# A guessed top-k threshold: its update rewritten over kept points, and GpSimd's copies cut in four

## What is computed

```python
def _topk_attention(Q, K, V, topk):          # 16 heads, d = 16, topk = 64
    scores = jnp.einsum('bhqd,bhkd->bhqk', Q, K) / jnp.sqrt(jnp.asarray(d, Q.dtype))
    topk_scores, topk_idx = jax.lax.top_k(scores, topk)
    probs = jax.nn.softmax(topk_scores, axis=-1)
    ...
x = x + tanh(g_xattn) * attention(layernorm(x), ctx, ctx)
x = x + tanh(g_ffn) * fp8_linear(layernorm(x))
```

## Time and profile before

| | us |
|---|---|
| median of 3 runs | 3022.32 |
| lowest, highest | 3021.08, 3029.27 |
| the profiled execution: its own time | 3019.36 |
| its span, first to last instruction | 3017.5 |
| VectorE busy in it | 2564.5 |
| ScalarE busy in it | 2500.6 |

### The profile page before, as it was taken

One profiled execution on the slowest core, in us unless ns is written; L12 is line 12 of the kernel. 1 busy time (PEld: TensorE's weight loads), 2 busy tenths in 40 slices (PEclk: granted clock), 3 DMA queues, 4 the chain that ended last, 5 costly groups with the idle time before them and its releaser, 6 DMA issues. The chain is left out here.

```text
span 3017.5 us, 56335 instructions
## 1 busy us (share of the span) xinstructions
PE 1434.2 (48%) x9104; PEld 920.2 (30%) x9104; DVE 2564.5 (85%) x10738; ACT 2500.6 (83%) x8774; POOL 1007.2 (33%) x1204
## 2 busy tenths in 40 slices
PE   3345555445544545433445445554445345445443
PEld 2123333333322333322333233332233233233321
DVE  1688899888989898888888889988988888898884
ACT  1679999799988899957989799998799699697982
POOL 5223343233434233422333334332343233232112
PEclk8556676666666776666766576766666676666656
DMA  4323333223333323232223333323233223232111
GB/s 69 48 39 64 61 57 59 49 57 63 68 57 52 62 57 63 55 54 42 54 56 66 57 65 56 63 57 61 53 61 64 44 52 63 46 65 44 36 37 33
DMA packets 451929, 166.76 MB, mean 55 GB/s; under 512 B 245616, under 2 KB 451440, under 8 KB 451520
## 3 DMA queue, kind: packets, MB, share of 16 engines
q1 hardware_dynamic: 451136, 162.38, 30.2%
q0 software_dynamic: 384, 0.33, 0.1%
HBM read 102.57 MB, written 59.24 MB: 54 GB/s over the span
## 5 line engine op out<-in xcount | busy, mean ns | idle before, releaser
L971 ACT ACTIVATE act_junk<-score_sb,X 128x256 int8<-128x256 f32 x3072 | 1522.1, 509 | 141.3 <-DVE X L1293 60.2
L971 ACT ACTIVATION_READ_ACCUMULATOR act_junk<-score_sb,X 128x1 f32 x3072 | 621.9, 202 | 0.0
L1006 ACT ACTIVATE unfit<-score_sb,thr 128x256 bf16<-128x256 f32 x1024 | 431.1, 514 | 169.5 <-DVEq L1444 169.5
L759 PE MATMUL ps_s<-ks,qs 96*128 96x256 bf16 x1024 | 231.8, 347 | 610.6 <-DVE score_sb L1179 600.6
L773 PE MATMUL ps_e<-qs,ks 99*128 99x256 bf16 x1024 | 348.9, 352 | 275.1 <-ACT unfit L1006 185.5
L1179 DVE TENSOR_SCALAR_CACHE_REDUCE score_sb<-ps_s 128x256 f32<-128x256 f32 x1024 | 397.9, 411 | 16.3 <-PE ps_s L759 10.8
L777 PE MATMUL ps_e<-dropb,unfit 128*128 128x128 bf16 x2048 | 350.4, 270 | 0.0
L1015 ACT ACTIVATE pT_sb<-ps_e 128x512 f32<-128x512 f32 x512 | 302.6, 592 | 51.6 <-PE ps_e L777 50.9
L794 PE MATMUL ps_o<-pT_sb,v_aug 128*32 128x256 f32 x2048 | 285.9, 499 | 110.2 <-ACT pT_sb L1015 59.2
L567 POOL CAST split<-proj 128x512 bf16<-128x512 f32 x64 | 46.5, 727 | 862.8 <-ACT proj L955 862.3
L1317 DVE TENSOR_SCALAR_CACHE_REDUCE masked<-score_sb,X 128x256 f32<-128x256 f32 x768 | 318.8, 470 | 13.9 <-DVE x_res L1497 8.4
(11 more groups left out here) (181 smaller groups left out, 3843.5 us busy)
## 6 DMA issues: line engine op xcount, KB each, us to landing
rows<-q_scr SPq DMA_DIRECT2D x192, 128.0 KB, 5.0
rows<-k_scr SPq DMA_DIRECT2D x192, 128.0 KB, 4.9
o_scr<-o_sb SPq DMA_DIRECT2D x128, 128.0 KB, 2.8
q_scr<-split SPq DMA_DIRECT2D x32, 384.0 KB, 2.7
k_scr<-split SPq DMA_DIRECT2D x32, 384.0 KB, 2.7
x_in<-in_x SPq DMA_DIRECT2D x32, 256.0 KB, 2.8
ctx_sb<-in_ctx SPq DMA_DIRECT2D x32, 256.0 KB, 3.0
v_scr<-proj SPq DMA_DIRECT2D x32, 256.0 KB, 5.9
```

The costliest lines, as they stand in the source:

```text
L759: ins = nc.tensor.matmul(ps_s[:, n % 2, jh * TOK:(jh + 1) * TOK], qs[u][0:SPLITS, h, 8 * jh:8 * jh + 8, :].rearrange("d j t -> d (j t)"), ...
L971: ins = nc.scalar.activation(act_junk[:, t % JUNK, :], score_sb[:, slot, t, :], ACT.Sign, scale=-1.0, bias=X[slot % 2][:, 0, t:t + 1], acc ...
L1006: ins = nc.scalar.activation(unfit[:, n % MASKS, jh, :], score_sb[:, slot, t, :], ACT.Relu, scale=-1.0, bias=thr[:, slot, t:t + 1])
```

## The change

The bracket and its tiles (`A`, `B`, `AB`, `above`, `below`, `far`, `both`) are gone. Instead each group keeps the three guesses and distances of its rounds (`guess`, one slot a round), and an update picks from these:

- round 0: three instructions; every row makes the Newton step, near rows too;
- round 1: ten; the chord through points 0 and 1 where they lie on both sides, else the Newton step from point 1; near rows move too;
- round 2: thirteen; the chord from point 2 to point 1 if that lies on the other side, else to point 0, else the Newton step. Rows near at point 2 keep it. The result is written straight into `following`, so the copy of line 1314 is gone.

A distance of round r has r times 2^-6 added (APART), so that two points never have equal distances. SLOPE goes from 0.0115 / 2 to 0.0123 / 2. The final tiles and the final counts wait for a semaphore of their own (`s_last`) and read the guess in `following`. The last step of round 2 has two waits ahead of it, for ScalarE's final counts and VectorE's picks of the group before.

GpSimd copies the operands by head in four pieces, each with 4 of the 16 blocks j of a row. The three small instructions of `prepare_rounding` that mark rows out of range (lines 1481, 1483, 1485) move from VectorE to GpSimd, behind its rounding (line 636) and ahead of the maxima's split; `finish` waits for them there (`s_nn`).

```diff
@@ -50,15 +50,17 @@
 AIM = 60.5
 WINDOW = 8
 START = 0.6745
-SLOPE = 0.0115 / 2
+SLOPE = 0.0123 / 2
 ROOT_BITS = 532487669.0
-NO_POINT = 1000.0
+APART = 2.0 ** -6
 WIDE = ((0, 1, 2, 3), (6, 7, 8, 9), (12, 13, 14, 15))
 NARROW = ((4, 5), (10, 11), ())
 HEADS = ((0, 1, 2), (3, 4, 5), (6, 7))
 QUARTER = 4
-FINAL_BEFORE = (0, 14, 27)
-FINAL = 45
+FINAL_BEFORE = (0, 13, 26)
+FINAL = 44
+PICKED = 41
+FCS = 4

...
@@ -123,21 +125,15 @@
         max8 = sb("max8", [P, 8])


-        X = [sb(f"X{k}", [P, 2, GT]) for k in range(2)]
-        A = [sb(f"A{k}", [P, 2, GT]) for k in range(2)]
-        B = [sb(f"B{k}", [P, 2, GT]) for k in range(2)]
-        AB = sb("AB", [P, 2, GT])
+        guess = [sb(f"guess{k}", [P, GUIDES, 2, GT]) for k in range(2)]
         count = [sb(f"count{k}", [P, GT]) for k in range(2)]
-        aim = sb("aim", [P, GT])
-        newton = sb("newton", [P, GT])
-        product = sb("product", [P, GT])
+        step = sb("step", [P, GT])
+        product = sb("product", [P, GUIDES, GT])
+        limits = sb("limits", [P, GUIDES, GT])
+        flags = sb("flags", [P, GUIDES, GT], I32)
+        across = sb("across", [P, GT], I32)
+        run = product[:, 0:2, :]
         chord = sb("chord", [P, GT])
-        square = sb("square", [P, GT])
-        above = sb("above", [P, 2, GT], I32)
-        below = sb("below", [P, 2, GT], I32)
-        far = sb("far", [P, GT], I32)
-        far_f = sb("far_f", [P, GT])
-        both = sb("both", [P, GT], I32)
...
@@ -510,7 +508,8 @@
             nc.gpsimd.memset(ones_c[:], 1.0).then_inc(s_id, 1)
             nc.gpsimd.memset(ones_r[:], 1.0).then_inc(s_id, 1)

-            nc.gpsimd.memset(aim[:], TOK - 2 * AIM).then_inc(s_id, 1)
+            nc.gpsimd.memset(limits[:, 0:2, :], 0.0).then_inc(s_id, 1)
+            nc.gpsimd.memset(limits[:, 2, :], (WINDOW - 1) ** 2 + 0.5).then_inc(s_id, 1)
...
-                nc.gpsimd.tensor_copy((qs, ks)[k][u][0:SPLITS].rearrange("d h j t -> d j h t"),
-                                      rows[:].rearrange("d j (h t) -> d j h t", t=D)).then_inc((s_qh, s_kh)[k], 1)
+                for j in range(0, NJ, NJ // 4):
+                    ins = nc.gpsimd.tensor_copy((qs, ks)[k][u][0:SPLITS, :, j:j + NJ // 4, :].rearrange("d h j t -> d j h t"),
+                                                rows[:, j:j + NJ // 4, :].rearrange("d j (h t) -> d j h t", t=D))
+                ins.then_inc((s_qh, s_kh)[k], 1)
...
                 nc.gpsimd.tensor_tensor(xq_sb[:], ysum_sb, magic_sb[:], ALU.subtract).then_inc(s_q, 1)
+                pool.wait_ge(s_nan, 2 * b + 2)
+                carry(pool)
+                nc.gpsimd.tensor_scalar(nanrow[:], rowmax[:], 464.0, 3.0e38, ALU.is_gt, ALU.mult).then_inc(s_nn, 1)
+                pool.wait_ge(s_nn, 3 * b + 1)
+                carry(pool)
+                nc.gpsimd.tensor_scalar(nanrow[:], nanrow[:], 3.0e38, None, ALU.mult).then_inc(s_nn, 1)
+                pool.wait_ge(s_nn, 3 * b + 2)
+                carry(pool)
+                nc.gpsimd.tensor_tensor(rowmax[:], nanrow[:], nanrow[:], ALU.subtract).then_inc(s_nn, 1)
...
-                                               bias=X[slot % 2][:, 0, t:t + 1], accum_out=count[slot % 2][:, t:t + 1])
+                                               bias=guess[slot % 2][:, r, 0, t:t + 1], accum_out=count[slot % 2][:, t:t + 1])
...
             def final_counts(i, slot, r, counted):

-                act.wait_ge(s_fin, FINAL * i + 1)
+                act.wait_ge(s_last, i + 1)
                 act.wait_ge(s_cnt, counted)
                 for t in NARROW[r]:
                     ins = nc.scalar.activation(act_junk[:, t % JUNK, :], score_sb[:, slot, t, :], ACT.Sign, scale=-1.0,
-                                               bias=X[slot % 2][:, 0, t:t + 1], accum_out=final_count[:, t:t + 1])
+                                               bias=following[:, t, 0:1], accum_out=final_count[:, t:t + 1])
...
                 nc.vector.tensor_reduce(variance[:], gauss_sq, AX.X, ALU.add).then_inc(s_st, 1)
-                nc.vector.memset(A[slot % 2][:], NO_POINT)
-                nc.vector.memset(B[slot % 2][:], -NO_POINT)
...
-                nc.vector.scalar_tensor_tensor(x[:, 0, :], sd[:], START, gauss_mean[:], ALU.mult, ALU.add).then_inc(s_st, 1)
+                nc.vector.scalar_tensor_tensor(guess[slot % 2][:, 0, 0, :], sd[:], START, gauss_mean[:], ALU.mult, ALU.add).then_inc(s_st, 1)
...
             def update_thresholds(i, slot, r):
-
-
-                x = X[slot % 2]
-                lo_side, hi_side = A[slot % 2], B[slot % 2]
-                off = x[:, 1:2, :].to_broadcast([P, 2, GT])
+                points = guess[slot % 2]
+                x, off = points[:, r, 0, :], points[:, r, 1, :]
                 dve.wait_ge(s_cnt, GT * (GUIDES * i + r + 1))
                 carry(dve)
-                nc.vector.tensor_tensor(x[:, 1, :], aim[:], count[slot % 2][:], ALU.subtract).then_inc(s_upd, 1)
+                nc.vector.tensor_scalar(off, count[slot % 2][:], -1.0, TOK - 2 * AIM + r * APART, ALU.mult,
+                                        ALU.add).then_inc(s_upd, 1)
                 yield
                 dve.wait_ge(s_upd, 1)
-                nc.vector.tensor_scalar(above[:], off, 0.0, None, ALU.is_gt)
-                nc.vector.tensor_scalar(below[:], off, 0.0, None, ALU.is_le)
-                nc.vector.tensor_tensor(square[:], x[:, 1, :], x[:, 1, :], ALU.mult)
-                nc.vector.scalar_tensor_tensor(newton[:], x[:, 1, :], SLOPE, spread[slot % 2][:], ALU.mult,
+                if r == 1:
+                    nc.vector.tensor_tensor(product[:, 2, :], points[:, 0, 1, :], off, ALU.mult)
+                    nc.vector.tensor_tensor(run, points[:, 1], points[:, 0], ALU.subtract)
+                if r == 2:
+                    nc.vector.tensor_tensor(product[:], points[:, :, 1, :], points[:, 2:3, 1, :].to_broadcast([P, GUIDES, GT]),
+                                            ALU.mult)
+                nc.vector.scalar_tensor_tensor(step[:], off, SLOPE, spread[slot % 2][:], ALU.mult,
                                                ALU.mult).then_inc(s_upd, 1)
                 yield
-                dve.wait_ge(s_upd, 2)
-                nc.vector.copy_predicated(lo_side[:], above[:], x[:])
-                nc.vector.copy_predicated(hi_side[:], below[:], x[:])
-                nc.vector.tensor_tensor(newton[:], newton[:], x[:, 0, :], ALU.add)
-                if r:
-                    nc.vector.tensor_scalar(far_f[:], square[:], (WINDOW - 1) ** 2 + 0.5, None, ALU.is_gt)
-                nc.vector.tensor_scalar(far[:], square[:], (WINDOW - 1) ** 2 + 0.5, None, ALU.is_gt).then_inc(s_upd, 1)
-                yield
-                dve.wait_ge(s_upd, 3)
-                ins = nc.vector.copy_predicated(x[:, 0, :], far[:], newton[:])
+                done = 2
+                dve.wait_ge(s_upd, done)
                 if r == 0:
-                    ins.then_inc(s_thr, 1)
+                    nc.vector.tensor_tensor(points[:, 1, 0, :], x, step[:], ALU.add).then_inc(s_thr, 1)
                     dve.sem_clear(s_upd)
                     return
-                nc.vector.tensor_tensor(AB[:], hi_side[:], lo_side[:], ALU.subtract).then_inc(s_upd, 1)
+                if r == 1:
+                    nc.vector.tensor_scalar(across[:], product[:, 2, :], 0.0, None, ALU.is_lt)
+                if r == 2:
+                    nc.vector.tensor_tensor(flags[:], product[:], limits[:], ALU.is_lt).then_inc(s_upd, 1)
+                    yield
+                    dve.wait_ge(s_upd, 3)
+                    nc.vector.copy_predicated(points[:, 0], flags[:, 1:2, :].to_broadcast([P, 2, GT]), points[:, 1])
+                    nc.vector.tensor_tensor(across[:], flags[:, 0, :], flags[:, 1, :], ALU.max).then_inc(s_upd, 1)
+                    yield
+                    dve.wait_ge(s_upd, 4)
+                    nc.vector.tensor_tensor(run, points[:, 2], points[:, 0], ALU.subtract).then_inc(s_upd, 1)
+                    yield
+                    done = 5
+                    dve.wait_ge(s_upd, done)
+                nc.vector.reciprocal(chord[:], run[:, 1, :])
+                nc.vector.scalar_tensor_tensor(run[:, 0, :], run[:, 0, :], -1.0, off, ALU.mult, ALU.mult).then_inc(s_upd, 1)
                 yield
-                dve.wait_ge(s_upd, 4)
-                nc.vector.reciprocal(chord[:], AB[:, 1, :])
-                nc.vector.tensor_tensor(product[:], AB[:, 0, :], lo_side[:, 1, :], ALU.mult)
-                nc.vector.scalar_tensor_tensor(both[:], AB[:, 1, :], -NO_POINT + TOK, far_f[:], ALU.is_gt,
-                                               ALU.mult).then_inc(s_upd, 1)
+                dve.wait_ge(s_upd, done + 1)
+                nc.vector.tensor_tensor(chord[:], chord[:], run[:, 0, :], ALU.mult).then_inc(s_upd, 1)
                 yield
-                dve.wait_ge(s_upd, 5)
-                nc.vector.tensor_tensor(chord[:], chord[:], product[:], ALU.mult).then_inc(s_upd, 1)
```

(59 more changed lines are left out.)

## The result

The changed kernel takes 2932.4 us (median of four runs, 2928.9 to 2938.8); the kernel before, on the same chip, 3023.4 us. The ratio is 0.9693, with a 95% interval of 0.9679 to 0.9707: 91 us, or 3.1%, faster. 176 us had been forecast. The sign and the range hold, the size is half.

The account below looks back on a forecast made before the run. A loop of VectorE from (1, 2) to (0, 2), PE, then ScalarE was taken to set the time. 4.3 us a batch (129 us) plus 45 us of selections off 3019.4 gave 2845, left at 2846 us; range 2765 to 2940.

Parts of the forecast that it names:

- What bounds it: Loop: VectorE from (1, 2) to (0, 2) and its copies, PE, then ScalarE to the counts of (1, 2).
- The update: VectorE's updates: round 0 0.77 us less, round 1 0.9 us less, round 2 0.0.
- the update and the memsets: Rounds (0, 0) 0.77 us and (0, 1) 0.9 us less, plus 0.1 us for two memsets dropped from `start_thresholds`.
- The pieces: Line 1335's pair, stalled by GpSimd's copy of the queries, takes 1.8 us: 2.9 us less in 26 rounds (0, 0).
- a new chance to be second: Two-input VectorE and SBUF-reading GpSimd instructions exclude each other; the one issued second waits for the whole other.
- the first rival: ScalarE leads other rounds too, or line 1335's pair meets two pieces: 2.0 us a batch, 2917 us; chance 0.17.
- the forecast's own bounds: 3.0 to 5.5 us saved a batch and 6 to 16 tiles selected exactly: 2775 to 2930 us.
- Two of the signs named for it: Signs that the forecast is right: a batch near 79 us, and ScalarE over 86% busy.
- One named against it: Sign that the forecast is wrong: instructions of round 2's update of 0.8 us beside GpSimd's split.
- The selections: Exact selections fall from 15 in 12 groups to 11 in 10, at 12.8 us plus 9.9 each further: 45 us less.

Follow-up runs that it names:

- the marks: Changed kernel with the three small mark instructions moved back from GpSimd to VectorE: 2930.7 us, ratio 0.9709.
- the halved exponentials: Changed kernel with ScalarE's exponentials over half of each tile, the other half of the probabilities left at zero: 2883.9 us, ratio 0.9545.
- the run at the old slope: Changed kernel with SLOPE back at 0.0115 / 2: 2963.0 us, ratio 0.9815.
- the pieces alone: Kernel before with GpSimd's copies in four pieces, nothing else: 3005.0 us, ratio 0.9949.
- both other traces that keep them: Kernel before with GpSimd's copies in four pieces, 3005.0 us; kernel before with 24 semaphore steps on GpSimd ahead of the queries' copy, 3029.5 us.

## Why the prediction was half right

**What bounds it: right, but for one round.** The prediction drew the loop from the waits, VectorE in three rounds and ScalarE from behind (0, 2) to the counts of (1, 2), and said that savings in the rounds of (1, 0) and (1, 1) only lengthen a wait. The table, the marks and the halved exponentials show it. The wait before (1, 2) went from 1.9 to 3.9 us. The one round is (0, 0), below. That PE carries the loop from VectorE to ScalarE was read from the queue's order, and no run tried it.

**The update: right by instruction, and its sum partly by luck.** Where no copy is beside it, the update of round 0 takes 0.56 us and that of round 1 1.58, 0.77 and 0.95 us less than before; round 2 gives nothing. But the sum counted the 0.9 us in round (0, 1), and there the update takes 0.3 us more than before. What came instead is in (0, 0): 2.8 us, with the copy cut or whole, because the pair of line 1335 gets ahead of it. So the 54 us forecast for the update and the memsets lie near the 59 and 70 us of the run at the old slope, without having been saved where the prediction had them.

**The pieces: the step that failed.** The prediction took 2.9 us in 26 rounds, 75 us. Measured: 15.7 us alone (25 with the selections equal), none beside the update. The stall was read rightly from the earlier trace rows, if in 23 rounds and not 26, and what a piece does to the pair nearly: 2.2 us and not 1.8, with the pieces alone. Two things were left out. The term was added to the update's 0.77 us as if both could be had, while the earlier update already takes the pair out of the copy's way. And the round was looked at alone: VectorE, come earlier to update (0, 1), meets the same copy there. The prediction had named this danger, each piece "a new chance to be second" and the new update's instructions with two inputs, but priced it in a rival and not in the sum. It belonged in the sum.

**ScalarE in the round (0, 0): underrated.** It has 0.7 us of wait for ScalarE at its end now, and caps what this round can give at about 2.8 us. This was the first rival at 2.0 us a batch and 2917 us, given 0.17. The result lies 15 us from it and 86 us from the forecast. The cause is that rival's in part. ScalarE is close behind, but leads in one round more and not in all. VectorE does meet the pieces again, but at update (0, 1) and not with the pair, which takes 1.73 us. The time of 2932 us lies just outside the forecast's own bounds, 2775 to 2930, and inside the range only because that took in parts of the rivals. Two of the signs named for it are missing: a batch takes 81.9 us and not about 79, and ScalarE is busy for 85% and not over 86. One named against it is there, a long instruction of round 2's update:

```profile
1613.28 0.96 DVE L1310 TENSOR_TENSOR following<-guess,step 128x16 f32<-128x16 f32 x1 [0.29 <-DVE step L1299]
```

It is over 0.5 us in 6 of 64 groups, and so costs little.

**The selections: right in kind, off in size.** 13, where 11 were taken, and 10.8 us each, where 12.8 was read. The 12.8 is the growth of the one round, and some 2 us of it come back in the rounds around it. The gain was 31 us by the total times, or two selections against the 15 of the trace, some 22 us; 45 had been forecast. The old rule and constants give 16 selections in both other traces that keep them, and 15 in that of the kernel before. The one that is missing there is in every other trace with selections. What makes it come and go was not tried.

## What to carry to other kernels

Where two engines hand each other work every round, sum a saving around the loop and not by instruction: it counts only in the rounds that the engine leads, and an edit that brings it forward changes what it collides with next. Two gains that act on one stall don't add. And where a branch depends on the data, count how often it is taken before polishing the code around it: a tile less on this branch is worth 10.8 us, about a sixth of the 59 to 70 us that the shorter update, 23 instructions fewer in each of the 64 groups with the memsets, brought together with what it moved.

## What the hardware showed that was not expected

The first instruction of an update, one input of 128x16, takes 0.14 us, and up to 0.94 us beside GpSimd's copy (line 1259 of the changed kernel). The prediction had looked for such stalls on instructions with two inputs, and of those with one input only on the copy of line 1314, which goes. The Trainium skill, page "SBUF — State Buffer", section "Who interferes with whom", lists `tensor_scalar` among the operations that can take the port pair shared with GpSimd, where their operands meet its conditions. This trace agrees, at 0.64 us for the update that starts at 1634.81.
